# Masks of the maxima in an eight-block transformer kernel: an identity matmul on TensorE, or a masked minimum per head on VectorE

## The reference, cut to what matters

```python
def _L3_attn_ref(x, Wq, Wk, Wv, Wo):
    ...
    scores = jnp.einsum('bkgqd,bkmd->bkgqm', qg, k) / np.sqrt(HEAD_DIM)
    causal = jnp.tril(jnp.ones((s, s), dtype=bool))
    scores = jnp.where(causal, scores, -jnp.inf)
    attn = jax.nn.softmax(scores, axis=-1)
    out = jnp.einsum('bkgqm,bkmd->bkgqd', attn, v)
```

## Time and profile before

| | |
|---|---|
| median of the runs | 2687.57 us |
| profiled execution, device time | 2694.11 us |
| its span, first to last instruction | 2692.4 us |
| TensorE busy | 2429.6 us (90%) |
| VectorE busy | 1493.0 us (55%) |
| ScalarE busy | 945.3 us (35%) |
| GpSimd busy | 567.3 us (21%) |
| mean granted TensorE clock | 0.941 of full |

### The profile page before, as it was taken

How to read it: one execution, slowest core, us unless ns; L and a number is a source line. 1 busy time by engine, 2 the same in 40 slices (tenths; PEclk the granted TensorE clock), 3 DMA queues, 4 the chain that set the end, 5 groups by cost and what they waited for, 6 DMA issues and landing times.

```text
span 2692.4 us, 35635 instructions
## 1 busy us (share of the span) xinstructions
PE 2429.6 (90%) x12720; PEld 1285.8 (48%) x12720; DVE 1493.0 (55%) x3183; ACT 945.3 (35%) x1781; POOL 567.3 (21%) x638
## 2 busy tenths in 40 slices
PE   6555567999999999999999999999996999999998
PEld 5333324555554545455555555555453444444443
DVE  6666667877675766657677777776871011111101
ACT  1221121555343544545454545455553001011000
POOL 0455422223221121313222222221321000000000
PEclk8666778999999999999999999999998999999999
DMA  5000033122030121312131213221204000010000
GB/s 159 4 4 3 6 113 104 52 77 90 25 110 30 38 78 32 105 52 89 33 113 33 90 32 105 79 90 41 97 26 149 0 0 16 0 47 0 16 0 16
DMA packets 90793, 144.89 MB, mean 54 GB/s; under 512 B 8577, under 2 KB 63873, under 8 KB 89345
## 3 DMA queue, kind: packets, MB, share of 16 engines
q1 hardware_dynamic: 90640, 142.91, 16.5%
HBM read 81.93 MB, written 52.56 MB: 50 GB/s over the span
## 4 chain that ended last, share of the span: by engine, by line
PE 54%; issue 24%; DVE 3%; DMA 1%; ACT 1%; POOL 0%; SPq 0%; POOLq 0%; DVEq 0%; ACTq 0%
PE ps L1253 8%; PE ps L1213 8%; PE ps L1195 8%; PE ps L1173 7%; PE ps L1232 6%; PE ps L1268 4%; PE ps L1158 4%; PE ps L1170 3%; PE ps L1300 2%; PE ps L1277 2%; DVE negmax L1934 1%; DMA scr_q<-big 1%; PE ps L1287 1%; PE ps L1181 1%; ACT big L1443 1%
## 5 line engine op out<-in xcount | busy, mean ns | idle before, releaser
L1934 DVE TENSOR_REDUCE negmax<-ps 128x1 f32<-128x512 f32 (+3 forms) x1056 | 646.6, 636 | 308.0 <-PE ps L1173 303.4
L1443 ACT ACTIVATE big<-ps 128x512 f32<-128x512 f32 (+1 forms) x1056 | 570.0, 560 | 653.8 <-PE ps L1195 631.9
L1643 POOL TENSOR_SCALAR_AFFINE_SELECT big<-big 128x512 f32<-128x512 f32 x384 | 256.8, 672 | 1065.8 <-ACT big L1443 1065.3
L1137 PE MATMUL ps<-xt,big 128*128 128x512 f32 x896 | 390.3, 598 | 3.4 <-ACT xt L1366 3.4
L1195 PE MATMUL ps<-big 99*128 99x512 bf16 (+3 forms) x1536 | 372.1, 302 | 10.8 <-DVE rest L2041 6.8
L1173 PE MATMUL ps<-big 96*128 96x128 bf16 (+3 forms) x1536 | 379.4, 302 | 0.0
L1253 PE MATMUL ps<-big,xt 128*128 128x512 f32 (+1 forms) x768 | 293.1, 487 | 1.0 <-ACT xt L1464 0.7
L1137 PEld LDWEIGHTS ps<-xt,big 128*128 128x128 f32 x896 | 171.8, 192 | 219.7 <-issue 219.7
L1170 PE MATMUL ps<-cbf 128*128 128x128 bf16 (+2 forms) x1056 | 259.5, 246 | 13.4 <-issue 12.1
L1213 PE MATMUL ps<-big,vs 128*32 128x512 f32 (+3 forms) x3072 | 247.7, 440 | 2.3 <-POOL big L1643 2.2
L1173 PEld LDWEIGHTS ps<-big 96*128 96x128 bf16 x1536 | 143.0, 98 | 204.1 <-issue 163.9
(11 more groups left out here) (218 smaller groups left out, 2684.2 us busy)
## 6 DMA issues: line engine op xcount, KB each, us to landing
big<-scr_q SPq DMA_DIRECT2D x96, 384.0 KB, 4.0
scr_q<-big SPq DMA_DIRECT2D x48, 384.0 KB, 2.8
scr_q<-big SPq DMA_DIRECT2D x48, 256.0 KB, 3.0
big<-scr_k SPq DMA_DIRECT2D x48, 192.0 KB, 3.6
r<-x SPq DMA_DIRECT2D x8, 1024.0 KB, 4.7
big<-in_ffn_gu SPq DMA_DIRECT2D x14, 512.0 KB, 8.8
scr_q<-big SPq DMA_DIRECT2D x48, 128.0 KB, 3.1
big<-in_attn_w SPq DMA_DIRECT2D x3, 1536.0 KB, 8.3
```

Source lines behind the costliest of these rows:

```text
L1137: mm = pe.matmul(ps[:, 2 * (m % 2) + k, :], w(c, m), xt[:, c, :], start=(c == 0), stop=(c == DC - 1))
L1443: act.activation(probs_of(i), bank_of("exp", g, i)[:, 0:len(heads) * w], ACT.Exp, scale=1.0 / 16 if attn_of(n) == 1 else 0.25).then_inc(ma ...
L1643: pool.affine_select(block_, block_, [[0, GQ], [1, P]], ALU.is_ge, zero, base=0, channel_multiplier=-1).then_inc(made["cut"], 1)
L1934: dve.tensor_reduce(negmax[:, p % 2, q, h0:h0 + n], bank_of("max", p, u)[:, 0:n * w].rearrange("p (h k) -> p h k", h=n), AX.X, ALU.max, ne ...
```

## The change

The identity matmul with the mask is gone; the first head's product clears the bank's flags in its place. On VectorE, `take_max` issues one instruction per head: it adds the table `above` (f32, 0 in its first 384 columns, the triangle of -1e30 and 0 in the last 128) to the head's scores, multiplies by -1, writes the result over the scores in PSUM, and gives the minimum as that head's entry of `negmax`. The last of a unit's instructions signals. The table is made once at the start, from the masks that a DMA brings anyway. The planner's costs follow.

```diff
@@ pieces
         last = [("DVE", "split", k[:1], 900)] if k[1] == 2 * UNITS - 1 else []
-        return [("PE", "max", k, columns(n * (P + w), 0.43)), ("DVE", "negmax", k, 190 + columns(n * w, 1.05))] + last
+        return [("PE", "max", k, columns(n * w, 0.43)), ("DVE", "negmax", k, n * (220 + columns(w, 1.05)))] + last
@@ program
+        above = sb("above", [P, S], F32)
@@ max_scores
                 bank = bank_for("max", p, u)[:, 0:n * w].rearrange("p (h k) -> p h k", h=n)
-                pe.matmul(bank[:, :, w - P:w], identb, mask_q.unsqueeze(1).broadcast_to((P, n, P)),
-                          start=True, stop=False, skip_group_check=True)
                 for k, h in enumerate(heads):
                     mm = pe.matmul(bank[:, k, :], qt[0:KROWS, g % 6, h, q * P:(q + 1) * P], kt[0:KROWS, p % 3, g % 2, 0:w],
-                                   start=False, stop=True, skip_group_check=True)
+                                   start=(k == 0), stop=True, skip_group_check=True)
                 mm.then_inc(made["max_full"], 1)
@@ take_max
-                dve.tensor_reduce(negmax[:, p % 2, q, h0:h0 + n],
-                                  bank_of("max", p, u)[:, 0:n * w].rearrange("p (h k) -> p h k", h=n),
-                                  AX.X, ALU.max, negate=True).then_inc(made["negmax"], 1)
+                bank = bank_of("max", p, u)[:, 0:n * w].rearrange("p (h k) -> p h k", h=n)
+                for k in range(n):
+                    last = dve.tensor_tensor_reduce(bank[:, k, :], bank[:, k, :], above[:, S - w:S], -1.0, 3e38, ALU.add, ALU.min,
+                                                    negmax[:, p % 2, q, h0 + k:h0 + k + 1])
+                last.then_inc(made["negmax"], 1)
@@ block of VectorE, start
             dve.memset(vs[:], 0.0).then_inc(clearing, 1)
+            dve.memset(above[:, 0:S - P], 0.0)
             dve.wait_ge(constants, 16)
+            dve.tensor_copy(above[:, S - P:S], t1[:, P:2 * P])
             dve.tensor_copy(cbf[:], t1[:, 0:3 * P]).then_inc(constants, 1)
```

## The result

The changed kernel takes **2692.94 us** (median of 17 runs, 2688.03 to 2700.58) beside 2685.08 us of the kernel before (17 runs, 2680.1 to 2694.42): ratio 1.0031, 95% interval 1.002 to 1.0043. The profiled run has a span of 2697.6 us, 5.2 us more than before.

What follows compares the result with a forecast made beforehand. TensorE was taken to bound the whole attention. Stretch gains less a 4 us loss at the start gave 73 us; less 18 us for delays left 55, so 2632 us from 2685.08, range 2606 to 2725.

Steps and rivals of the forecast that it cites:

- the rival of the cheap instruction: VectorE's new masking instruction has the old reduction's fixed cost, 0.063 us: 78 us gained, 2610 us; chance 0.13.
- I price that at nothing, plus or minus 10 us: Planner costs change with the edit, so every engine's order of work changes; effect taken as zero, within 10 us.
- 82 us for the mask matmuls: TensorE in attention: removing 1056 mask matmuls saves 0.86 us per group of four heads, at most 82 us over 96 groups.
- So nothing is to be had there from the clock: TensorE's granted clock was already 1.00 (2.4 GHz) in all attention stretches but the first, so no gain was expected from it.
- f = 0.15: Fixed start-to-start cost in us of VectorE's new per-head instruction, against 0.063 before; adds 164 us of VectorE time in all.
- I let VectorE be busy for 95% at most: Each attention stretch lasts the longer of TensorE's need and VectorE's busy time over 0.95; net gain 73 us.
- The 18 us for fuller queues: Longer VectorE items delay TensorE: 9 us more for maxima in the chain, another 9 or so for other VectorE work.
- The views of waits say that this is no larger: TensorE waited only 20.3 and 13.0 us for VectorE's reductions, so the queueing loss was held to be no larger.
- The masks don't leave the path: Rival: something else on TensorE's path, weight load or exponentials, is late at once; perhaps no change, 2685 us; chance 0.09.
- A: Experiments' theory: VectorE's added time, meeting other work at the handover between sequences, stalls TensorE, and its clock falls afterwards.
- B: Experiments' theory: the mask matmuls were not worth their 80 us on TensorE's path.
- C: Experiments' theory: the planner's two new cost numbers re-made the work order on all engines, and this order is worse by itself.

## Why the prediction was wrong, step by step

The forecast summed to -55 us; the medians differ by +8. The table splits the 63 us between them: the removal brought 54 where 78 was the sum with nothing added (the rival of the cheap instruction), 24 short; VectorE's half cost 38 where 78 - 55 = 23 was meant, 15 more; the order cost 24 where nothing was meant. 24 + 15 + 24 = 63. Along the other way through it, first the order (+42), then the removal (-52), then VectorE's half (+18), the parts are other ones and the sum is the same.

- **"I price that at nothing, plus or minus 10 us" (the order): the step that failed most.** It is worth 24 us in the changed kernel, 42 and 44 in its neighbours, and decides the sign alone: with the planner's line left as it was, or with the instruction's measured cost, the same change is 0.9 or 0.7% faster than before. Of the 44 us without masks, 16 come with TensorE's lower cost (2647 against 2631) and 28 with VectorE's 220 ns for each head.
- **82 us for the mask matmuls: right as work, not as time.** In the order of before and without masks, the work at full clock falls by 1551.5 - 1474.6 = 77 us. But TensorE's idle time grows by 5 and the lost clock by 15, which leaves 58 of profiled span. VectorE had nothing added there, so these 15 us of clock, and the 24 us by which the removal falls short, are not the price of its new work.
- **"So nothing is to be had there from the clock": read one way only.** The clock couldn't rise above 1.00, but it could fall, and 41 us of the changed kernel's loss are that. I had the first stretch's 0.96 in the earlier trace rows before me and didn't ask what it followed.
- **f = 0.15: a little high (0.115 to 0.117).** The trace agrees with what VectorE: DVE Perf Modes of the Trainium skill (§ Two Vector instructions with no wait between them) says: an operation that writes out its accumulator is two instructions, here with a second record of 141 ns. The estimate of 0.15 with about 75 ns for each, from Vector Engine (DVE) Microarchitecture Reference (§ 5.2) of the Trainium skill, was too high: the second adds 0.116 - 0.063 = 0.053 us. The measurement decides.
- **"I let VectorE be busy for 95% at most" and the sum by stretch: failed.** VectorE's busy times came out at 106.6, 436.7, 457.9 and 186.3 us, each below the forecast's, and no stretch was VectorE's. The limit isn't in an average over 130 to 600 us but in some 10 us once for each sequence, where VectorE was already full in the kernel before. Adding to an engine that works in order is paid there first: 18 us for a quarter of the pairs in both orders, against 0 and 9 for another quarter.
- **The 18 us for fuller queues** were of the right kind and too small, since they left the clock out: VectorE's half cost 38 us in the order of before. In the profiled spans it is 33, of which 15 are idle time (39.1 to 54.3), 12 clock (26.4 to 38.0) and 7 work, which is within the error of that column.
- **"The views of waits say that this is no larger": failed.** They show who waited for the maxima. A step further lie the exponentials, held up in ScalarE's queue by a late remainder: 9.5 us at the handovers in place of 0.8. The larger part of the waits for ScalarE (81.2 us) comes from the removal and the order. The sentence on what would show the prediction wrong was right, though: the idle time ahead of lines 1172 and 1194 grew with VectorE under 90%, latency and the order, not the load.
- **The rivals.** f of 0.34 and half rate are out by rows. "The masks don't leave the path" had nearly the right time for another reason: they left it, and the order and the handover took their place. Of the theories, A holds for the place (18 us against 0 or 9), not for the size; B falls with the 54 us of the removal alone; C holds for the order of the change, which is slower under all three sets of instructions.

**What stays open.** Why the higher cost makes an order in which ScalarE's exponentials come late was not followed through the planner. The new order also raises the work at full clock by 11.5 us in the kernel before (1551.5 to 1563.0), little more than the 8 us by which that column differs between runs of the same TensorE instructions. And that idle time causes the lower clock is argued from their succession; it was not tried by itself, and its length alone doesn't decide. In the changed kernel with the order of before, TensorE stood still for 2.81 us in one piece, and the clock stayed at 1.00 (columns of the second fence as in the earlier trace rows):

```profile
1524.42 0.39 PE L1180 MATMUL ps<-cbf,shp 128*24 128x128 bf16 x4 [2.81 <-DVE negmax L1935]
```

```profile
1520.00:1525.00 5.00, 2.19 (x17) 1.51 (x17) 4.93 (x12) 1.29 (x3) 5.00 (x5) 1.00 0.00 0
1525.00:1530.00 5.00, 5.00 (x40) 4.12 (x40) 4.02 (x18) 1.51 (x4) 0.34 (x1) 1.00 0.04 11
```

The run without masks and with measured costs has such a stop of 3.00 us at 792 us, also with no fall behind it, while some falls of the run without masks in the order of before come behind 1.2 us in 5 (at 1086 us), as much as the kernel before stood at its handovers without one.

## What to carry to other kernels

Where a planner sets the order, a change of its costs is a change of its own: run it apart from the instructions (the first two rows of the table above need only two kernels more), since it can be worth more than they are. Before adding to an engine that works in order, look for the 5 us slices in which it is full, not for its share of a stretch, and ask whose queue stands behind it. And the best edit here was one that adds nothing: softmax doesn't need the maximum of the allowed keys, any number near it will do, so the masks of the maxima could go without replacement, for 2631 us in the order of before, 2% below both kernels, as long as no forbidden product is so much larger that the exponentials of the allowed ones vanish.

## What the runs showed of the hardware

- TensorE's granted clock fell from 1.00 to about 0.5 for some 7 us behind handovers where TensorE had been idle for 1.3 to 2.2 us in 5, in pieces of up to 0.64 us at the one shown, in stretches in which it is busy for 95 to 98%. It mostly cost 3.4 us at a time, and 41 us more than in the kernel before. But 1.2 us were followed by a fall in one run and by none in the kernel before, and single stops of 2.81 and 3.00 us in two other runs by none: these runs give no length of idle time that decides it.
- The accumulating VectorE instruction is two records (707 and 141 ns at 512 columns), 0.053 us more start to start than a plain reduction, with its result written back to the bank at no visible cost: 1.04 ns a column in both (start to start, (0.65 - 0.25)/384 us for the new one).
- How often the clock falls differs between runs of one kernel: the one whose handover had been relieved went from 2662.6 us at a mean clock of 0.939 to 2683.1 at 0.932. A profile of one run can be off its median by 13 us for that reason.
